# Scan distance 8 to 4 in a two-layer graph kernel, and its first layer's last tile gathered and summed in three parts

## What is computed

```python
h = relu(layernorm(x))
Qn, Kn = cos_normalize(h @ Wq.T), cos_normalize(h @ Wk.T)
att = softmax(where(adj > 0, Kn @ Qn.T, NEG), axis=1)
x = x + 0.5 * (att @ h) + 0.5 * h        # h alone where a row has no neighbour
h = relu(layernorm(x))
g = h @ W.T + b_W
e = leaky(g @ a1 [:, None] + g @ a2 [None, :] + b_a)
x = x + softmax(where(adj > 0, e, NEG), axis=1) @ g
```

## Time and profile before

| | us |
|---|---|
| median of 3 runs | 1599.63 (1599.62 to 1599.75) |
| the profiled execution's own time | 1598.47 |
| its span (first to last instruction) | 1596.6 |
| POOL busy | 1101.7 (69%) |
| PE busy | 1102.4 (69%) |
| DVE busy | 993.2 (62%) |
| ACT busy | 970.0 (61%) |
| mean granted TensorE clock | 0.840 of 2.4 GHz |
| `adj` loads, share of the 16 DMA engines' time | 43.0% |

### The profile page before, as it was taken

How to read it: one execution, slowest core, us unless ns; L and a number is a source line. 1 busy time by engine, 2 the same in 40 slices (tenths; PEclk the granted TensorE clock), 3 DMA queues, 4 the chain that set the end, 5 groups by cost and what they waited for, 6 DMA issues and landing times.

```text
span 1596.6 us, 22567 instructions
## 1 busy us (share of the span) xinstructions
PE 1102.4 (69%) x6257; PEld 873.3 (55%) x6257; DVE 993.2 (62%) x4076; ACT 970.0 (61%) x2806; POOL 1101.7 (69%) x1137
## 2 busy tenths in 40 slices
PE   6887778887777788787765366556656665656666
PEld 4663555555554565555565355545555555555655
DVE  6977679887898787888875243444344434444444
ACT  5663778778877787877789544444444444444432
POOL 2247677677777777777676377777777777777774
PEclk9997889998999888999877677787777777787777
DMA  9998999999999999999922122222222222222221
GB/s 366 424 395 340 411 376 404 410 406 366 391 407 408 356 405 405 407 395 407 381 54 54 39 57 60 60 61 59 61 60 60 59 61 60 59 61 59 61 61 44
DMA packets 90988, 359.56 MB, mean 225 GB/s; under 512 B 23909, under 2 KB 36584, under 8 KB 58088
## 3 DMA queue, kind: packets, MB, share of 16 engines
q1 hardware_dynamic: 49128, 277.05, 43.0%
q0 software_dynamic: 34816, 72.49, 17.7%
q10 hardware_dynamic: 6912, 8.52, 1.5%
HBM read 345.25 MB, written 12.72 MB: 224 GB/s over the span
## 4 chain that ended last, share of the span: by engine, by line
POOL 44%; issue 17%; DMA 16%; PE 9%; ACT 8%; DVE 5%; SPq 0%; ACTq 0%; POOLq 0%; DVEq 0%
POOL arena L519 19%; DMA arena<-in_adj_dram 15%; POOL arena L514 13%; POOL arena L940 7%; POOL arena L946 5%; ACT prod L1166 3%; PE ps L990 3%; PE ps L1015 3%; ACT diag L1185 1%; DMA arena<-tab,idx_shared 1%; PE ps L971 1%; PE ps L1027 1%; ACT R L1136 1%; ACT R L1138 1%; ACT R L1134 1%
## 5 line engine op out<-in xcount | busy, mean ns | idle before, releaser
L940 POOL DMA_INDIRECT arena<-tab,idx_own x320 | 329.3, 1029 | 142.2 <-issue 90.8
L519 POOL DMA_INDIRECT arena<-tab,idx_own x320 | 302.2, 944 | 97.5 <-issue 97.5
L990 PE MATMUL ps<-arena,fold 128*128 128x512 fp8e4 x1024 | 279.7, 409 | 95.1 <-DMA arena<-in_adj_dram 94.5
L535 PE MATMUL ps<-ident,arena 128*128 128x128 f32 x704 | 147.4, 385 | 209.4 <-DMA arena<-tab,idx_shared 209.4
L514 POOL DMA_INDIRECT arena<-tab,idx_shared x224 | 214.2, 956 | 96.8 <-issue 68.0
L946 POOL DMA_INDIRECT arena<-tab,idx_shared x224 | 217.3, 970 | 68.3 <-issue 68.3
L535 PEld LDWEIGHTS ps<-ident,arena 128*128 128x128 f32 x704 | 130.2, 281 | 222.5 <-DMA arena<-tab,idx_shared 222.5
L587 ACT ACTIVATE arena<-arena,negm 128x517 f32<-128x517 f32 (+1 forms) x64 | 56.8, 887 | 277.2 <-DVE negm L653 277.2
L990 PEld LDWEIGHTS ps<-arena,fold 128*128 128x128 bf16 x1024 | 91.0, 99 | 242.1 <-DMA arena<-in_adj_dram 134.5
L1166 ACT ACTIVATE prod<-prod,arena 128x128 f32<-128x128 f32 x544 | 210.3, 391 | 0.4 <-ACT s_all L402 0.4
L643 DVE SCALAR_TENSOR_TENSOR arena<-ps,s_all,arena 128x512 f32<-128x512 f32 (+1 forms) x112 | 66.9, 634 | 205.3 <-PE ps L535 205.3
(11 more groups left out here) (186 smaller groups left out, 2432.2 us busy)
## 6 DMA issues: line engine op xcount, KB each, us to landing
arena<-in_adj_dram SPq DMA_DIRECT2D x256, 1024.0 KB
arena<-tab,idx_own POOLq DMA_INDIRECT x640
arena<-tab,idx_shared POOLq DMA_INDIRECT x448, 2.6
tab<-arena ACTq DMA_DIRECT2D x16, 260.0 KB, 7.6
tab<-tw ACTq DMA_DIRECT2D x32, 130.0 KB
res<-in_x_dram SPq DMA_DIRECT2D x8, 512.0 KB, 11.7
out_dram<-arena SPq DMA_DIRECT2D x64, 64.0 KB, 1.6
prod<-in_L_gnn_Wq_dram SPq DMA_DIRECT2D x1, 64.0 KB
```

The source lines that it names most:

```text
L519: pool.indirect_dma_start(out=GO[q][:, s, :], out_offset=None, in_=tab1, in_offset=bass.IndirectOffsetOnAxis(ap=idx_own[:, t, s:s + 1], ax ...
L535: last = nc.tensor.matmul(T_ps[c // 4][:, c % 4 * P:(c % 4 + 1) * P], GS[h % 2][:, first + c, D:D + 1].to_broadcast([P, P]), ident[:, :], ...
L940: pool.indirect_dma_start(out=G[q][:, s, :], out_offset=None, in_=tab0, in_offset=bass.IndirectOffsetOnAxis(ap=idx_own[:, t, s:s + 1], axi ...
L990: last = nc.tensor.matmul(keys_ps[t % 2], fold[:, PIECE_BITS * f + b, :], ring8[m % RING][:, b * WORDS:(b + 1) * WORDS], start=False, stop ...
```

## The change

1. `LAGS` goes from 8, 7, 6, 5 (falling at tiles 14, 28, 42) to 8, 7, 6, 5, 4 (falling at tiles 12, 24, 36, 48). Four turns have no fold now (PE's 3, 16, 29, 42), three had (5, 20, 35), and the last tile is folded in turn 58 and not in 57. `decode` and `compact` in one turn are kept for the pairs with the shortest lag, 24 to 31 now and 21 to 31 before.
2. In a turn, `owners(t+1)` on PE goes from the beginning to the end. On ACT `copy_owners(t)` comes first and `masks(t+2)` comes before the diagonals. On DVE `select(t)` is done in turn t behind the products and ahead of `extract`, where `select(t+1)` was done behind `extract`.
3. Tile 63: POOL gathers its shared chunks first, then own slots 0 to 2, then 3 and 4 with a semaphore of their own. Products, scores, exponents and diagonals are made in these three parts, and PE waits for two parts of the diagonals.
4. All eight first masks of the second layer are made behind the first layer.

```diff
-        LAGS = ((14, 8), (28, 7), (42, 6), (T, 5))
+        LAGS = ((12, 8), (24, 7), (36, 6), (48, 5), (T, 4))
...
-        soon = {i for i in range(LEAD + 1, PAIRS) if lag(2 * i) == 5}
+        soon = {i for i in range(LEAD + 1, PAIRS) if lag(2 * i) == 4}
...
+                def gather_own(t, first, end, landed):
...
+                for t in range(T - 1):
+                    if t >= GR:
+                        pool.wait_ge(s_pv, t - GR + 1)
+                    gather_own(t, 0, K, s_g[0][t % GR])
+                    gather_shared(t)
+                pool.wait_ge(s_pv, T - GR)
+                gather_shared(T - 1)
+                gather_own(T - 1, 0, 3, s_g[0][(T - 1) % GR])
+                gather_own(T - 1, 3, K, s_last)
...
                 for t in range(-1, T):
-                    if t + 1 < T:
-                        owners(t + 1)
                     if t in (0, 1):
                         folds(AHEAD + 2 + t)
...
                     if scan >= AHEAD + 4:
                         folds(scan, PIECES // 2, PIECES)
+                    if t + 1 < T:
+                        owners(t + 1)
...
-                weighted(T - 1)
+                weighted_last(T - 1)
...
-                for t in range(-1, T):
+                for t in range(T):
+                    copy_owners(t)
...
-                    if t + 1 < T:
-                        copy_owners(t + 1)
                     if t >= 2:
-                        weights(t - 2)
+                        scores(t - 2, 0, slots(t - 2))
+                        exps(t - 2)
+                    if t + 2 < T:
+                        masks(t + 2)
+                    if t >= 2:
+                        diags(t - 2)
                     if t % 2 == 0 and t >= 8:
                         second.scalar_h(act, (t - 8) // 2)
-                    if t + 3 < T:
-                        masks(t + 3)
-                    if t == T - 4:
-                        act.wait_ge(s_piece, PIECES * T)
-                    if t >= T - 4:
-                        masks1_scalar(act, t - T + 4)
...
-            for t in range(QT, AT1):
+            for t in range(AT1):
                 masks1_scalar(act, t)
...
+                    if t >= 0:
+                        select(t)
...
                     if t in scanned:
                         extract(scanned[t])
-                    if t + 1 < T:
-                        select(t + 1)
```

More of the change, by code:

```diff
@@ L904, in adjacency_layers @@
         assert scanned[0] == AHEAD + 2 and len(scanned) == T - AHEAD - 2
-        assert all(t <= 2 * i - 3 for at in (placed, placed_soon) for t, i in at.items())
+        assert all(t <= 2 * i - 2 for at in (placed, placed_soon) for t, i in at.items())
         with nc.Block() as block:
@@ L933, in _, with gather_shared @@
                     pool.wait_ge(s_tst[p], 16 * (NB // HR))
-                for t in range(T):
-                    q = t % GR
-                    if t >= GR:
-                        pool.wait_ge(s_pv, t - GR + 1)
+                def gather_own(t, first, end, landed):
                     pool.wait_ge(s_own, t // 2 + 1)
-                    for s in range(K):
+                    for s in range(first, end):
                         pool.indirect_dma_start(
-                            out=G[q][:, s, :], out_offset=None, in_=tab0,
+                            out=G[t % GR][:, s, :], out_offset=None, in_=tab0,
                             in_offset=bass.IndirectOffsetOnAxis(ap=idx_own[:, t, s:s + 1], axis=0),
-                            bounds_check=None).then_inc(s_g[0][q], 16)
+                            bounds_check=None).then_inc(landed, 16)
+                def gather_shared(t):
                     pool.wait_ge(s_idx, t + 1)
@@ L1031, in weighted, with weighted_last @@
                     last.then_inc(s_pv, 1)
+                def weighted_last(t):
+                    p, q, n = t % 2, t % GR, PAIRED[t % QT]
+                    pe.wait_ge(s_W, paired(t + 1))
+                    pe.wait_ge(s_fin, t - 1)
+                    for j in range(n):
+                        v, s, e = shared(t, SPAN[t % QT][0] + j)
+                        nc.tensor.matmul(pv_ps[p][:, 0:ROW], W[p][j], Gc[:, e, :], start=j == 0, stop=False)
+                    for part, (a, b) in enumerate(((0, 3), (3, K))):
+                        pe.wait_ge(s_dg, t + 1 + part)
+                        for s in range(a, b):
+                            last = nc.tensor.matmul(pv_ps[p][:, 0:ROW], diag[t % DR][:, s, :], G[q][:, s, :], start=False,
+                                                    stop=s == K - 1)
+                    last.then_inc(s_pv, 1)
                 def offsets_after(i):
@@ L1254, in _ @@
                 second.scalar_rows(act, PAIRS - 5)
+                last_scores(T - 1, K, slots(T - 1), 1)
+                last_exps(T - 1, K, slots(T - 1), 3, 1)
                 second.scalar_root(act, PAIRS - 3)
                 second.scalar_hT(act, PAIRS - 4)
-                scores(T - 1, 0, K)
+                last_scores(T - 1, 0, 3, 2)
+                last_exps(T - 1, 0, 3, 6, 2)
+                last_diags(T - 1, 0, 3, 2)
                 second.scalar_h(act, PAIRS - 3)
                 second.scalar_rows(act, PAIRS - 4)
-                scores(T - 1, K, slots(T - 1))
-                exps(T - 1)
+                last_scores(T - 1, 3, K, 3)
+                last_exps(T - 1, 3, K, 8, 3)
+                last_diags(T - 1, 3, K, 3)
                 second.scalar_hT(act, PAIRS - 3)
                 second.scalar_root(act, PAIRS - 2)
-                diags(T - 1)
                 second.scalar_rows(act, PAIRS - 3)
@@ L1529, in _, with last_own_products @@
                         link(nc.vector.tensor_scalar(some_all[:, :], cnt_all[:, :], 0.0, None, ALU.is_gt))
+                def last_own_products(t, first, end, landed, n):
+                    dve.wait_ge(landed, n)
+                    nc.vector.tensor_tensor(prod[t % 2][:, first:end, :], G[t % GR][:, first:end, 0:D],
+                                            repeat(owner[:, t, 0:D], end - first), ALU.mult).then_inc(s_prod, 1)
                 second.vector_stats(dve, link, PAIRS - 4)
```

32 lines of the change are left out of this document (28 added, 4 removed).

## The result

The changed kernel takes 1582.7 us (median of 6 runs, 1579.3 to 1584.7). The kernel before took 1599.6 us beside it (6 runs, 1592.2 to 1600.3). The ratio is 0.990, with a 95% interval of 0.9885 to 0.9915, so the gain of 16 us is clear of the noise. The profiled execution took 1584.06 us with a span of 1582.3.

The account below looks back on a forecast made before the run. The second layer's first gather, set by the scan's end (DMA engines full) plus an ACT-bound tail, was to move from 899.9 to 803.3 + 79.8 = 883.1, -16.8 us, giving 1583 us; range 1576 to 1593.

Parts of the forecast that it names:

- Term 1: Start of the scan: tile 8's fold goes behind owners(0), so ring slots come free 6 us sooner; -5.3 us.
- Term 2: Scan turns without a fold: four at 2.5 us each, 10.0 us lost against 9.0 before; +1.0 us.
- Term 3: End of scan: last tile folded a turn later, one more tile's gathers share the DMA engines; +2.2 us.
- Rival 2: Scan: POOL becomes the bound, standing for `select`; last fold slips by up to 10.5 us, 1594 us; chance 0.08.
- Rival 4: Scan: distance 4 too short, PE waits 10 us and more for counts in eight pairs; 1614 us; chance 0.09.
- My signs of being wrong: In the scan: POOL waiting over 30 us for `select`, or PE waiting for counts in the last eight pairs.
- Term 4: Last fold to second layer's first gather: less work and shorter waits on ACT; 94.5 becomes 79.8 us.
- The parts of tile 63: First layer's end: +0.9 us on ACT; split sum gives nothing by itself, `hT` and its projection precede the last sum.
- The clock: Tail: PE's array halves its clock when idle, so twelve-matmul owners stay at 3.45 us; upper clock gives 1577.
- the likeliest case: Whole kernel: the forecast alone, between 1577 (upper clock) and 1588 us (turns without a fold at their bound); chance 0.62.

## Why the prediction was right, and where it was not

The time came out as forecast, 1583 against 1582.7, inside 1576 to 1593, on the side of faster. That it is right to 0.3 us is luck: the runs themselves scatter by 5 us, and the steps did not all hold. The prediction's "last fold" is the fold of the last piece (805.41 before).

- **Term 1, the start, -5.3 us.** Right in mechanism and size. The fold of tile 8 stands at 121.5, the share there is 0.98, and undone it costs 5.3 us by the ratios (3.2 at the last fold in the profile).
- **Term 2, four turns without a fold, 10.0 us of loss.** Right in size. The windows from 300 to 340, 460 to 500 and 620 to 640 us, and 0.98 at 160 to 180, have lost about 2.9, 1.6, 2.0, 0.2, 3.5 and 0.8 us against 1.02, together 11.0. The places are 5 to 40 us later than forecast.
- **Term 3, one tile more, +2.2 us, and with it the last fold at 803.3.** The number can't be called wrong. The last piece was folded from 806.05 in the changed kernel's profile, and from 802.9 to 804.6 in the three others with the same scan. The mechanism failed. "On POOL the same gathers cost 10.5 us of its 43.6 us of waits, which covers them" was the wrong sentence. The 43.6 us for PE did fall to 7.2, but 53.0 us for `select` came in their place. The sum has no term for the path of landing, products and `select`, which together with DVE's full turn filled two turns in the last part of the scan. Cutting it brought the last piece's fold to 800.3, even earlier than 803.3.
- **Rival 2**, POOL that waits for `select`, at 0.08, was the right mechanism. It does not cost the 10.5 us that I gave it. Cutting the loop brings 4.5. I had looked at POOL's time per turn (10.5 of 12) and not at the path from a gather's landing through DVE back to POOL, nor at DVE's own time in the turn in which it decodes.
- **Rival 4**, PE waits for the counts, came as well (60.7 us, 18 times), but not as I had it. In the eight pairs at distance four PE waited 2.1 to 4.4 us seven times and once not at all, against "10 us and more in each of the eight pairs". With these counts moved, the time stays the same, so their price is nothing. And the distance is not the reason: with distance five in the new order PE waits 85.1 us.
- My signs of being wrong, over 30 us of waits for `select` and waits for counts in the last pairs, both appeared, and the time was right nonetheless. A wait that replaces another is a sign of where the bound has gone, and no price.
- **Term 4, the tail, 94.5 to 79.8 us.** It measured 80.0. That is luck in part, for the parts were mis-sized and cancel. One tile less behind the last fold is worth 9.5 us, most of a turn, where I had 7.3 from ACT's busy time. The masks of the second layer are worth 1.9 in the tail (4.8 by the ratio), where I had 7.0, because ACT had idle time for part of them. What remains of the 14.4 for the place of the masks and the order is 3.0, where I had 2.3; but the masks put back behind the diagonals cost 4.4 of tail alone, so the parts do not simply add. ACT's waits for owners are 4.7 us (5.4 forecast). From the last sum (874.21 + 1.13) to the first gather it is 10.7 (11.1 forecast). The masks stay hidden in the second layer: its first exponent comes 14.6 us behind its first gather, 14.5 before.
- **The parts of tile 63** give nothing (0.9901 without them). The reason that I gave, `hT` and its projection ahead of the last sum, is only a part of it: with both out of the way PE is still at the sum of the tile before.
- **The clock.** Owners of twelve matmuls took 3.30 and 3.06 us in the tail, at a granted clock of 0.54 and 0.57, after waits of 5.8 and 4.4 us, against 1.84 at full clock. Over the whole stretch from the last fold to the last diagonals the clock was 0.79, so PE was at the upper level for more than half of it. But the owners that ACT waits for fell into the lower level, and the 4.8 us did not come. By these 4.8 the lower edge of the likeliest case was 1578 and not 1577.
- **The noise.** "Runs of this kernel agree to 0.01%" came from three runs. Six runs of the kernel before span 8 us, 0.5%.

On the landing in the loop there is a figure to weigh. The Trainium skill (Perfetto Trace Analysis, on the DMA instruction of the software path) says that the interval shown on GpSimd ends when the descriptors are written, not when the data has arrived. The trace agrees: 0.94 us is shown, and the rows are used 4.9 us after it. The Trainium skill (DMA: Bandwidth & Descriptors, on the anatomy of one DMA) puts the fixed part of a DMA at about 2.0 us. Measured from a gather's start to its landing, it is 5.6 us (median) while `adj` is loaded, and 2.9 behind the scan, when the DMA share is 0.2 to 0.3. An estimate with that page's 2.0 would make the loop 3.6 us shorter than it is; the measurement decides.

## What to carry to other kernels

When lists, masks or buffers are moved a turn nearer, don't only count each engine's work in a turn. Follow each loop once round (issue, landing, products, selection, next issue) and compare its length with the turn: here POOL had 1.5 us of 12 to spare in a turn, while the loop took 10.2 to 11.5 us in one turn and DVE alone 13.8 in the next. Where turns differ, compare the sum over the whole period, here two turns. Put the operation that releases another engine ahead of one that waits for a transfer, where it doesn't need that transfer. A stage that an experiment makes earlier is worth nothing until the time at the end has moved: the folds ended ten us sooner in one kernel, with no gain. And ask of a wait that appears which part of the change brought it, by undoing one part: here it was the order and not the distance.

## What the runs showed of the hardware

- A gather's landing, from its start: 5.6 us (median, up to 6.5) while the `adj` loads fill the DMA engines, and 2.6 to 3.7 us (median 2.9) behind them.
- One program ran in 1597.6 us on one chip and 1922.2 us on another, at a clock of 0.84 and 0.77. In a profile from the second PE's weight loads stood for up to 52 us at a time. Orders that differ by less than 1% can't be compared there.
- The same second layer took between 696.2 and 699.3 us from its first gather on in the kernels here, so a difference of 3 us in one profile's span is not yet a difference. The same scan ended between 803.9 and 807.1 us.
